# State space block: two of batch 0's six convolution tiles filtered on GpSimd instead of VectorE

## What is computed

```python
zxbcdt = _rms(x, norm_w) @ in_proj_w            # 256 -> z 512 | xBC 768 | dt 8
z, xBC = zxbcdt[..., :512], zxbcdt[..., 512:1280]
dt = softplus(zxbcdt[..., -8:] + dt_bias)
padded = pad(xBC, 3 tokens ahead)
conv = conv_b + sum(padded[:, k:k + L, :] * conv_w[:, k] for k in range(4))
xBC = silu(conv)                                # xh 512 | B 128 | C 128
# per token: h = h * exp(dt * A) + dt * xh x B;  y = h . C + D_skip * xh
u = _rms(y * silu(z), gnorm_w)
x = x + u @ out_proj_w
```

## Time and profile before

| | us |
|---|---|
| median of 3 runs | 978.45 (977.73 to 978.66) |
| the profiled execution | 977.36 |
| span of its instructions | 975.5 |
| TensorE / VectorE / ScalarE / GpSimd busy | 867.4 / 526.4 / 449.3 / 46.4 |

### The profile page before, as it was taken

One profiled execution on the slowest core, in us unless ns is written; L12 is line 12 of the kernel. 1 busy time (PEld: TensorE's weight loads), 2 busy tenths in 40 slices (PEclk: granted clock), 3 DMA queues, 4 the chain that ended last, 5 costly groups with the idle time before them and its releaser, 6 DMA issues.

```text
span 975.5 us, 10834 instructions
## 1 busy us (share of the span) xinstructions
PE 867.4 (89%) x4452; PEld 407.7 (42%) x4452; DVE 526.4 (54%) x714; ACT 449.3 (46%) x672; POOL 46.4 (5%) x39
## 2 busy tenths in 40 slices
PE   3887799989999999987699999999778998889987
PEld 2433344443444444535233625433345433554342
DVE  3367999923343103134653505358949677794552
ACT  3564222274343414424244262457776367863534
POOL 0000000030000000000220000000002000220000
PEclk9999899997979999996799699899979999899999
DMA  9000000000000000030000000000000000000011
GB/s 379 22 1 0 1 0 0 0 1 1 0 2 1 0 1 0 1 127 2 0 1 1 2 1 2 1 1 0 1 0 2 1 0 0 2 1 1 1 44 44
DMA packets 3005, 15.62 MB, mean 16 GB/s; under 512 B 656, under 2 KB 912, under 8 KB 2320
## 3 DMA queue, kind: packets, MB, share of 16 engines
q1 hardware_dynamic: 2816, 12.88, 3.3%
q0 software_dynamic: 144, 2.10, 0.5%
HBM read 12.87 MB, written 2.10 MB: 15 GB/s over the span
## 4 chain that ended last, share of the span: by engine, by line
PE 72%; DVE 13%; ACT 12%; issue 2%; DMA 1%; DVEq 0%; SPq 0%; POOL 0%; ACTq 0%
PE ps L405 70%; ACT AR L619 3%; DVE VB L632 3%; ACT AR L1726 1%; ACT AR L1716 1%; DMA CX<-in_ctxT 1%; DVE AR L1993 1%; DVE VB L1858 1%; DVE AR L503 1%; PE ps L578 1%; DVE AR L1855 1%; DVE AR L644 1%; DVE AR L1854 1%; ACT AR L624 1%; ACT AR L622 0%
## 5 line engine op out<-in xcount | busy, mean ns | idle before, releaser
L405 PE MATMUL ps<-AR,WA 128*128 128x512 f32 (+3 forms) x780 | 339.8, 597 | 12.4 <-DVE AR L2222 3.6
L405 PEld LDWEIGHTS ps<-AR,WA 128*128 128x128 f32 (+2 forms) x780 | 143.5, 190 | 195.1 <-issue 181.6
L405 PE MATMUL ps<-AR,CN 128*128 128x512 f32 (+3 forms) x320 | 116.6, 627 | 7.8 <-DVE AR L498 4.5
L405 PE MATMUL ps<-AR 128*64 128x128 f32 (+5 forms) x680 | 99.8, 411 | 8.0 <-DVE AR L1993 2.6
L644 DVE TENSOR_TENSOR AR<-ps,AR 128x512 f32<-128x512 f32 x24 | 16.6, 692 | 105.1 <-ACT AR L624 105.1
L405 PEld LDWEIGHTS ps<-AR 128*64 128x64 f32 (+4 forms) x680 | 54.3, 166 | 45.6 <-issue 19.7
L619 ACT ACTIVATE AR<-ps 77x2048 f32<-77x2048 f32 x24 | 44.0, 1869 | 60.6 <-PE ps L405 60.6
L405 PEld LDWEIGHTS ps<-AR,CN 128*128 128x128 f32 (+2 forms) x320 | 40.3, 168 | 61.7 <-issue 39.5
L632 DVE TENSOR_REDUCE VB<-ps 128x16 f32<-128x1232 f32 x32 | 45.0, 1440 | 34.8 <-PE ps L405 34.8
L405 PE MATMUL ps<-KB,WA 128*128 128x512 f32 (+1 forms) x120 | 54.1, 619 | 2.8 <-ACT AR L1709 2.8
L2119 DVE SCALAR_TENSOR_TENSOR AR<-AR,VC 128x512 f32<-128x512 f32 x72 | 50.6, 749 | 5.3 <-ACT AR L1652 4.4
(11 more groups left out here) (318 smaller groups left out, 1085.3 us busy)
## 6 DMA issues: line engine op xcount, KB each, us to landing
WA<-in_m SPq DMA_DIRECT2D x1, 2856.0 KB, 9.6
WA<-in_m SPq DMA_DIRECT2D x1, 2560.0 KB, 15.4
X<-in_xT POOLq DMA_DIRECT2D x1, 2048.0 KB, 9.1
WA<-in_m SPq DMA_DIRECT2D x1, 2048.0 KB, 20.3
out<-X SPq DMA_DIRECT2D x4, 512.0 KB, 3.1
WB<-in_m SPq DMA_DIRECT2D x1, 1024.0 KB, 22.2
AR<-in_rows SPq DMA_DIRECT2D x1, 640.0 KB, 9.7
WA<-in_m SPq DMA_DIRECT2D x1, 512.0 KB, 16.2
```

Source lines behind the costliest of these rows:

```text
L405: return nc.tensor.matmul(out, lhsT, rhs, start=first, stop=last)
```

## The change

For batch 0, the first three taps of tiles 4 and 5 are taken from VectorE. GpSimd makes each as a product into EF[1]'s tiles 2 and 3 and an addition to CV, six of each per half, in the piece "in" of tile 5. ScalarE's "ef" for batch 1 waits until they are done, since it overwrites those tiles, and so does the Silu of batch 0. The setting of the three first columns of XB raises a semaphore of its own, which GpSimd waits for.

```diff
-            (("o6c", 2 * B), ("cv0", 6 * J)),
+            (("o6c", 2 * B), ("cv0", 4 * J)),
...
             for piece, b, j, s in mamba_order():
-                if piece == "s1":
+                if piece == "in" and b == 0 and s == 5:
+                    pool.wait_ge(sem("past"), B * j + 1)
+                    if j:
+                        pool.wait_ge(*after("x41", j))
+                    pool.wait_ge(*after(of("iev", 0), 10 * j + 6))
+                    for tap in range(TAPS - 1):
+                        for k in (4, 5):
+                            if tap:
+                                pool.wait_ge(sem("tapped"), 6 * j + 2 * tap + k - 5)
+                            nc.gpsimd.tensor_scalar(EF[1][:, k - 2, :], XB[0][:, k, tap:tap + T], v("convw", 4 * k + tap), None, ALU.mult).then_inc(sem("tap"), 1)
+                        for k in (4, 5):
+                            pool.wait_ge(sem("tap"), 6 * j + 2 * tap + k - 3)
+                            nc.gpsimd.tensor_tensor(CV[0][:, k, :], CV[0][:, k, :], EF[1][:, k - 2, :], ALU.add).then_inc(sem("tapped"), 1)
+                elif piece == "s1":
...
                     def convolved(b):
-                        act.wait_ge(*after(of("cv", b), XBC * (j + 1)))
+                        act.wait_ge(*after(of("cv", b), (XBC if b else 4) * (j + 1)))
+                        if b == 0:
+                            act.wait_ge(sem("tapped"), 6 * (j + 1))
...
                     act.wait_ge(*after(of("ef_mm", b), j + 1))
+                    if b:
+                        act.wait_ge(sem("tapped"), 6 * (j + 1))
...
                 dve.wait_ge(*after(of("iev", b), 10 * j + first + 2))
                 if first == 4 and j == 0:
                     nc.vector.tensor_copy(HIST[b], XB[b][:, :, T:T + TAPS - 1])
+                if first == 4 and b == 0:
+                    return
...
                         dve.wait_ge(*after(of("x4", b), j))
-                        ch.link(nc.vector.tensor_copy(XB[b][:, :, 0:TAPS - 1], HIST[b]))
+                        nc.vector.tensor_copy(XB[b][:, :, 0:TAPS - 1], HIST[b]).then_inc(sem("past"), 1)
+                        dve.wait_ge(sem("past"), B * j + b + 1)
                     elif s == 0:
-                        ch.link(nc.vector.memset(XB[b][:, :, 0:TAPS - 1], 0.0))
+                        nc.vector.memset(XB[b][:, :, 0:TAPS - 1], 0.0).then_inc(sem("past"), 1)
+                        dve.wait_ge(sem("past"), B * j + b + 1)
```

## The result

The changed kernel takes 993.92 us in the median (993.58 to 995.51, 4 runs), the kernel before 978.16 in the same series: 1.0164 times as long, with a 95% interval of 1.0147 to 1.0182, so 15.8 us slower. The forecast was 988.0 with a range up to 1000, slower with 0.82.

What follows compares the result with a forecast made beforehand. The prediction took TensorE, with ScalarE after it, to bound the kernel. Gain 0, plus 6.8 us in the second half and 2.7 in the first, made 9.5 us slower: 988.0 us, range 978.7 to 1000.

Steps and rivals of the forecast that it cites:

- What bounds, and the gain of zero: Whole kernel: TensorE, then ScalarE, hold the chain; VectorE's convolution is hidden, so removing its taps gains 0 in both halves.
- The second half's wait: Second half, ScalarE before batch 1's exponentials: GpSimd ends at 820.1 against a latest harmless 813.27, so 6.8 us late.
- The prices: GpSimd's new instructions undisturbed: 1.25 us a product, 1.1 an addition, 14.1 us a half, bounds 12.5 to 15.3.
- the wait beside VectorE: Second half: nine GpSimd operations each wait one VectorE instruction, 0.75 us, making 17.3 us for the nine.
- the first rival: Not slower: GpSimd runs undisturbed near the low price bounds and ends inside the budget; 977.7 to 978.7 us, 17%.
- TensorE's clock: Second half, matmuls after TensorE's idle 7 us near 817: the forecast sum had no term for a lower clock.
- The first half: VectorE's step sizes and small operations: twelve holds of 0.5 us, 6.0 in all, less slack, make TensorE's selection 2.7 us late.
- the slack: First half, before TensorE's selection matmul: grows from 0.55 to 3.35 us as VectorE's small operations end earlier.
- The sign named for this half: First half: TensorE's selection matmul would be 2 to 3 us late, released by VectorE.
- Starvation: Both halves: GpSimd works only in VectorE's pauses, 16.4 and 13.7 us late; 1008.6 us, 13%.
- a gain: Rival of a faster kernel: TensorE or ScalarE profits from earlier VectorE work, at most 2.8 us in the first half; 975.6 us, 3%.
- wide bound for the contention: Upper end of the contention case, 13.6 us late in the second half and 6.9 in the first; case 981.6 to 999, 67%.

Runs made afterwards that it cites:

- the kernel with the first half alone: Against the changed kernel, GpSimd makes the taps in the first half only, VectorE all of them in the second; 982.53 us, 1.0063 of the kernel before.

## Why the prediction was right, and where its sizes were off

**What bounds, and the gain of zero.** Right. The chain showed VectorE's convolution nowhere, and leaving the taps out changed the ratio to 1.0001 (0.9985 to 1.0017).

**The second half's wait.** Right in mechanism and place; that the size came out within 0.2 us is luck. The threshold was worked out as 13.96 us from tile 5's write; GpSimd needed 20.9 (807.12 to 828.06), against 20.8 forecast (799.31 to 820.1). TensorE waited 7.0 us, against 6.8. Two terms in it were wrong and made up for each other. The prices were too low: 1.25 forecast for a product and 1.10 for an addition, 1.56 and 1.27 measured alone. The fault is in taking a value below half a 1024-wide product: the 2.83 us of the earlier trace rows halved give 1.42, and the measured price is above that, as it is for the addition (1.27 above the 1.13 of a quarter of the 2048-wide one). Both fit a fixed part in each instruction, which the prediction named and then took to be outweighed by the overlap with VectorE. And the wait beside VectorE was too high: 0.75 us an operation forecast; in nine operations after the first three it was (20.7 - 16.6) / 9 = 0.46. With the measured prices a half is 16.6 us undisturbed, so even the first rival's "no contention" would have been 2.6 us late. That rival was dead by price, and the earlier trace rows came near to telling it: the halves as read there, 15.3 us, are above the 13.96 already.

**TensorE's clock.** This step failed: the clock was put at nothing without a reason. The prediction had a 7 us pause of TensorE in it and costed the work behind it at full clock. It was 3.0 us in the second half (shown by keeping TensorE busy), and about 1.8 in the first half of the changed kernel. The second is argued from rows, not shown, and the waits alone do not decide it: the kernel with the first half alone has the same waits and kept its clock.

**The first half.** Mechanism right, size short: 2.7 forecast, 4.7 by the waits. Two terms: VectorE was held by 7.45 us and not 6.0 (0.62 for each of twelve operations, not 0.5); and the slack was taken at `lparts` as 3.35 us, where the first to be late was ScalarE's exponential and the tile behind it, with the 2.8 us of the taps removed and none besides. 7.45 - 2.8 is the 4.7 measured. The sign named for this half, a selection matmul released by VectorE, did not come: it stood behind TensorE's own late matmuls. Even the 2.8 us reach `lparts` only in part: with the taps left out, the last operation of the row started 2.1 us earlier from the squares than before (24.95 and 27.05 us), as VectorE then waited 0.57 us for an exponential of ScalarE. The rule for such a step: each consumer in the row has its own slack, and the smallest counts.

**The rivals.** Starvation did not happen: GpSimd went on beside VectorE's stream, its pairs of the second half taking 1.6 to 2.1 us an operation. Nor did a gain show anywhere.

**The sum.** Forecast 6.8 + 2.7 = 9.5; by the cuts 7.2 + 4.7 by waits and 3.1 + 1.8 by the clock, 16.8, with 15.8 in the medians. Of the 7.3 us that were missing 4.9 are the clock, 2.0 the first half's waits and 0.4 the second's. The range held the result through its wide bound for the contention (999), not through a term for what was missing.

## What to carry to other kernels

Work moved off an engine that is not in the chain gained nothing here, and its new home had to fit in a budget that is read from the first instruction which waits for it: here a borrowed buffer put that instruction 7 us earlier in ScalarE's queue than the result itself did. When a forecast has TensorE idle for some microseconds (7 here), count as a case of its own what the matmuls behind it cost at the lower clock (3.1 us here). For GpSimd beside VectorE, price both: its own instruction alone, and the time by which its reads hold up VectorE's two-input operations.

## What the runs showed of the hardware

GpSimd's reads cost VectorE more than they cost GpSimd. In the first half twelve operations grew by 22.1 - 16.6 = 5.5 us and held VectorE up by 7.45, in the second by 4.1 and 7.3; single taps took up to 1.76 us instead of 0.75. What matters is the kind of access: beside GpSimd's memsets VectorE's two-input taps and scans kept their 749 and 406 ns, while two one-input tensor_scalar operations from SBUF, one of each, grew from 0.43 and 0.48 to 1.18 and 1.25 us, and the memsets beside them from 0.95 to 1.22 us. The Trainium skill, SBUF — State Buffer, section Who interferes with whom, says both, that two-input operations contend only with a GpSimd operation that reads, and operations in the two-port mode, which it says tensor_scalar can enter, with any; these rows agree, though none shows the mode itself. Its lock, held by one side for an instruction with the other fully blocked, would be too strong for the stream as a whole. Both went on, GpSimd at three quarters of its pace alone or a little more (16.6 of 22.1 and of 20.7 us), the taps of the second half at five sixths of theirs (749 of 905 ns in the mean). And in the 22.1 us of the first half there fitted GpSimd's 16.6 us and two-input work of VectorE that takes about 12 us undisturbed (an estimate from the rows before: 2.7 us of taps, then 2.35, 4.31, 0.69, 0.69 and 1.37), which is more than the two could have done in turns.
